# Attention over a full adjacency matrix: three bias-times-weight products on GpSimd, weight maxima by slices

## The chip, the cores and the metric

The kernel runs on one core of a Trainium2 chip. The metric is device time in microseconds (us) of one execution; lower is better.

## What is computed

```python
h = jnp.maximum(_layernorm(x, axis=-1), 0.0)
q = h @ Wq.T + bq;  k = key @ Wk.T + bk;  v = value @ Wv.T + bv
scores = jnp.einsum('nd,md->nm', q, k) / 64
adj_scores = scores * adj
adj_scores = jnp.where(jnp.abs(adj_scores) < 1e-05, -1e9, adj_scores)
prob = softmax(adj_scores, axis=-1)
out = x + jnp.einsum('nm,md->nd', prob, v) @ Wm.T + bm
```

x, key and value are 4096 x 512, adj is 4096 x 4096, the weights are 512 x 512, all fp32. The biases have 512 elements.

## The kernel before

**The algebra.** Keys and values are never projected. The start makes A = Wq^T Wk (`A_sb`) and B = Wv^T Wm^T (`B_sb`), so that a query row is h A plus a bias, multiplied directly by the keys, and an output row is (prob value) B plus a bias. Three products carry the biases: bq Wk is added to every query row (`qbias`), bk Wq is multiplied by the row (`wrow`, read by `row_dot`), bv Wm^T is added to bm (`obias`). A fourth, scalar one is bq bk (`once`, kept as `qk`). fp32 operands of the large products are split into two fp16 halves, high by ScalarE (`key_high`, `high_of`), low by VectorE (DVE; `key_low`, `low_of`), and multiplied three times (`split_product`, L559 to L561). The halves are scaled by powers of two that come from the largest element: DVE reduces each partition, TensorE flattens the column (`flat_max`), DVE reduces it again (`widest`), for keys GpSimd takes the root (`root_of`), TensorE spreads it to all partitions (`spread_max`), DVE makes the scales.

**The bias products before.** ScalarE's queue loads bq, bk, bv as columns of four per partition, and bm to all partitions (`obias`). DVE fills 12 blocks of 128 columns with repeated bias values (`bqrep`, `bkrep`, `bvrep`, L1053 to L1055), and TensorE multiplies four of them with the four 512-column slices of a weight (L695, L709, L663; L699 for the scalar). fp32 products run as two passes each, a product of four parts as eight.

**The order.** Work on every engine is written out by hand. After the start, one step t is one tile of 128 rows by 512 keys: TensorE makes the scores, DVE applies adjacency (L1225), ScalarE takes absolute values, DVE masks and keeps the maximum (L1285, L1234). Probabilities follow `LAG_P` = 9 steps later and are split, transposed by DMA (`pT`), and multiplied with the values from step `LAG_V` = 11 on. Eight steps make a block of rows, and there are 32 blocks. Steps 0 to 18 also do the rest of the preparation: the keys of groups 2 to 7 (steps 0 to 5), the transposing of Wm (`WM_STEP` 4), squares of the values on ScalarE for their maximum (up to step 7), the bv product (`BIAS_STEP` 5), B in four rounds (steps 6 to 9), the scale of values and B (`VB`, steps 7 and 8), the splitting of values (steps 8 on) and of B (`B_OUT` 10). The first product with values waits for the low half of B's first pair, since both use the bank.

**Queues.** Instructions of an engine run in the order written. SP issues nearly all loads in order, then waits for the step's events. GpSimd does `rstd_of` (three small operations for a row block), roots, the first row's units, a fourth of the values' scaling (L541) and low halves (L546), and the addition of `obias` to x (L550).

## Time and profile before

| | |
|---|---|
| runs (3) | 1592.18 us median, 1591.77 to 1592.73 |
| profiled execution | 1591.07 us |
| its span, first to last instruction | 1589.3 us |
| mean granted TensorE clock | 0.997 |
| TensorE busy | 1567.6 us, 99% |
| DVE, ScalarE, GpSimd busy | 993.6, 609.3, 101.8 us |
| DMA in the first 40 us, the next 40 us | 348, 254 GB/s |

The profile is of one execution. In the page's picture of 40 slices of 40 us, TensorE is below nine tenths in the first two slices and the last one only, and GpSimd is busy to a tenth to three tenths in slices 2 to 4 and idle elsewhere. A wait names what came last before the engine went on; "issue" is a wait that the profile can't name.

### The profile page before, as it was taken

To read this page: it belongs to the slowest core of one execution; us is meant where nothing else is said; L and a number is where in the kernel's file an instruction comes from. 1 tells how busy PE (TensorE), PEld (TensorE's weight loads), DVE (VectorE), ACT (ScalarE), POOL (GpSimd) and SP (SyncE) were. 2 spreads that over 40 slices of the span, in tenths; PEclk is the share of its full clock that TensorE was granted. 3 is DMA by queue.
4 is the path that set the end of the run, shared out by engine and by line. 5 is a ranking of instruction groups with operands and counts; after the bars stand their busy time and mean duration, and the time that the engine had idled before them with its cause. 6 is when DMAs were issued, how large, how long until landed. Compare 5 with 4: busy or idle time off the path is not lost.

```text
span 1589.3 us, 23599 instructions
## 1 busy us (share of the span) xinstructions
PE 1567.6 (99%) x7246; PEld 720.3 (45%) x7246; DVE 993.6 (63%) x2325; ACT 609.3 (38%) x964; POOL 101.8 (6%) x178
## 2 busy tenths in 40 slices
PE   8899999999999999999999999999999999999998
PEld 5543444444444444444444444444444444444443
DVE  4779766656666656656665656666566666666652
ACT  4667333333333333333333333333333333333332
POOL 0132000000000000000000000000000000000000
PEclk9999999999999999999999999999999999999999
DMA  9724555655555455555545555545555554555545
GB/s 348 254 53 107 121 130 117 130 126 125 119 125 124 116 136 119 124 125 127 117 116 137 119 123 122 130 120 119 135 123 119 121 129 119 126 129 124 116 95 106
DMA packets 430287, 205.46 MB, mean 129 GB/s; under 512 B 375088, under 2 KB 375344, under 8 KB 430128
## 3 DMA queue, kind: packets, MB, share of 16 engines
q1 hardware_dynamic: 429680, 204.80, 54.2%
q8 instruction: 16, 0.26, 0.1%
q10 hardware_dynamic: 576, 0.27, 0.1%
q14 instruction: 15, 0.12, 0.0%
HBM read 105.13 MB, written 8.39 MB: 71 GB/s over the span
## 4 chain that ended last, share of the span: by engine, by line
PE 93%; DVE 2%; DMA 2%; issue 1%; ACT 1%; SPq 1%; POOL 0%; DVEq 0%; ACTq 0%; POOLq 0%
PE R L559 13%; PE R L560 13%; PE R L561 13%; PE S L559 13%; PE S L560 13%; PE S L561 13%; PE M L559 3%; PE M L561 3%; PE M L560 3%; DMA pT<-ph 1%; PE R L638 1%; PE R L671 0%; DMA xq<-in_x_dram 0%; DVE small L1142 0%; PE W L709 0%
## 5 line engine op out<-in xcount | busy, mean ns | idle before, releaser
L941 ACT ACTIVATE drop<-Zbuf 128x512 f32<-128x512 f32 x256 | 161.2, 630 | 808.4 <-DVE cmx L1234 808.3
L1225 DVE SCALAR_TENSOR_TENSOR Zbuf<-S,rs,adjb 128x512 f32<-128x512 f32 x256 | 192.0, 750 | 346.4 <-PE S L561 342.6
L559 PE MATMUL R<-Vbuf,pT 128*128 128x512 f16 x1008 | 383.0, 380 | 6.9 <-issue 5.5
L560 PE MATMUL S<-Kbuf,qT 128*128 128x512 f16 x1024 | 388.9, 380 | 0.0
L559 PE MATMUL S<-Kbuf,qT 128*128 128x512 f16 x1024 | 388.8, 380 | 0.0
L561 PE MATMUL S<-Kbuf,qT 128*128 128x512 f16 x1024 | 388.7, 380 | 0.0
L560 PE MATMUL R<-Vbuf,pT 128*128 128x512 f16 x1008 | 382.9, 380 | 0.0
L561 PE MATMUL R<-Vbuf,pT 128*128 128x512 f16 x1008 | 382.8, 380 | 0.0
L1234 DVE CUSTOM_DVE_ANT_0 Zbuf<-drop,Zbuf 128x512 f32<-128x512 f32 x256 | 175.8, 687 | 0.0
L1285 DVE TENSOR_SCALAR drop<-drop,rs 128x512 f32<-128x512 f32 x256 | 142.1, 555 | 33.4 <-ACT drop L941 33.1
L947 ACT ACTIVATE Zbuf<-Zbuf,smx 128x1024 f32<-128x1024 f32 x128 | 157.4, 1230 | 4.5 <-DVE smx L1248 1.6
L559 PEld LDWEIGHTS R<-Vbuf,pT 128*128 128x128 f16 x1008 | 98.8, 98 | 128.0 <-issue 6.8
L559 PEld LDWEIGHTS S<-Kbuf,qT 128*128 128x128 f16 x1024 | 100.3, 98 | 121.4 <-issue 1.8
L561 PEld LDWEIGHTS S<-Kbuf,qT 128*128 128x128 f16 x1024 | 100.4, 98 | 121.3 <-issue 0.8
L560 PEld LDWEIGHTS S<-Kbuf,qT 128*128 128x128 f16 x1024 | 100.3, 98 | 121.3 <-issue 1.9
L561 PEld LDWEIGHTS R<-Vbuf,pT 128*128 128x128 f16 x1008 | 98.8, 98 | 119.6 <-issue 1.1
L560 PEld LDWEIGHTS R<-Vbuf,pT 128*128 128x128 f16 x1008 | 98.8, 98 | 118.8 <-issue 0.8
L1269 DVE SCALAR_TENSOR_TENSOR ph<-Zbuf,ph 128x512 f16<-128x512 f32 x130 | 90.0, 693 | 3.7 <-ACT ph L925 3.7
L925 ACT ACTIVATE ph<-Zbuf 128x512 f16<-128x512 f32 x130 | 81.8, 629 | 20.5 <-DMA pT<-ph 8.2
L1269 DVE SCALAR_TENSOR_TENSOR osb<-Zbuf,osb 128x512 f16<-128x512 f32 x122 | 83.4, 683 | 1.8 <-ACT osb L925 1.8
L494 POOL TENSOR_TENSOR small<-small,fixed 128x1 f32<-128x1 f32 x32 | 6.4, 201 | 1187.0 <-DVE small L989 1187.0
L925 ACT ACTIVATE osb<-Zbuf 128x512 f16<-128x512 f32 x122 | 75.0, 615 | 1.9 <-DMA pT<-osb 1.9
(189 smaller groups left out, 1194.2 us busy)
## 6 DMA issues: line engine op xcount, KB each, us to landing
adjb<-in_adj_dram SPq DMA_DIRECT2D x256, 256.0 KB, 2.8
xq<-in_x_dram SPq DMA_DIRECT2D x32, 256.0 KB, 2.8
Kbuf<-in_L_gnn_key_dram SPq DMA_DIRECT2D x8, 1024.0 KB, 14.3
xr<-in_x_dram SPq DMA_DIRECT2D x32, 256.0 KB, 2.8
out_dram<-xr SPq DMA_DIRECT2D x31, 256.0 KB, 2.3
Vbuf<-in_L_gnn_value_dram SPq DMA_DIRECT2D x7, 1024.0 KB, 8.8
pT<-ph SPq DMA_TRANSPOSE x130, 3.1
pT<-osb SPq DMA_TRANSPOSE x122, 3.1
```

Of the source, the lines that this page charges most:

```text
L494: nc.gpsimd.tensor_tensor(rstd[:, 0:1], mv[:, 1:2], eps[:, :], ALU.add).then_inc(var_ready, 1)
L559: nc.tensor.matmul(ps, lhs[0], rhs[0], start=start, stop=False)
L560: nc.tensor.matmul(ps, lhs[0], rhs[1], start=False, stop=False)
L561: return nc.tensor.matmul(ps, lhs[1], rhs[0], start=False, stop=stop)
L638: last = nc.tensor.matmul(bank_of(fill + s)[:, :], Wv_sb[:, k, s * P:(s + 1) * P], WmT[:, k, :], start=(k == 0), stop=(k == ND - 1))
L925: nc.scalar.activation(rows_p(s)[:, 0, :], probs_of(u), ACT.Copy, scale=PSCALE).then_inc(p_hi, 1)
L941: nc.scalar.activation(drop[:, :], Zbuf[:, s.p, s.c * CW:(s.c + 1) * CW], ACT.Abs).then_inc(abs_ready, 1)
L947: nc.scalar.activation(at, at, ACT.Exp, bias=smx[:, pp, 2 * NPAIR + 1:2 * NPAIR + 2], scale=smx[:, pp, NPAIR + k:NPAIR + k + 1], accum_out ...
L1225: nc.vector.scalar_tensor_tensor(out=z, in0=S[s.j % 2][:, :], scalar=rs[:, r, 3, s.c // 2:s.c // 2 + 1], in1=adjb[:, s.j % ADJ_SLOTS, :], ...
L1234: nc.vector.tensor_tensor_reduce(out=last, in0=drop[:, :], in1=last, scale=1.0, scalar=-3.4e38, op0=ALU.add, op1=ALU.max, accum_out=cmx[:, ...
L1269: nc.vector.scalar_tensor_tensor(out=rows_p(s)[:, 1, :], in0=probs_of(u), scalar=PSCALE, in1=rows_p(s)[:, 0, :], op0=ALU.mult, op1=ALU.sub ...
L1285: nc.vector.tensor_scalar(drop[:, :], drop[:, :], rs[:, r, 1, s.c // 2:s.c // 2 + 1], rs[:, r, 2, s.c // 2:s.c // 2 + 1], ALU.is_lt, ALU.m ...
```

## The change

The bias rows are loaded each as one piece of 2 KB into one partition. TensorE turns them into columns by 12 products of one column, and DVE copies these to `bqc`, `bkc`, `bvc`. For each of the three bias products GpSimd multiplies the four slices of the weight by the bias column and adds them up (`weighted_sum`: four multiplications, three additions of 128x512), and TensorE sums the result over the partitions with one product by ones (`sum_over_partitions`), which also spreads it. The scalar product is made on DVE from the columns and summed in the same way. The first sum and three slices of the second stand on GpSimd ahead of `root_of("K0")`, the last slice behind it; the third sum stands in step 5, behind DVE's reading of Wm, and writes over Wm. The bv product moves from step 5 to step 9 on TensorE, with its addition to `obias` on DVE. Warming products go from 20 to 12. DVE reads the maxima of Wq and Wk slice by slice as these land. The rest of the row preparation, and of TensorE's order in the start, is moved as the diff shows. Two adjacency loads go ahead of keys 2 to 7, and the load of bm goes from ScalarE's queue to SP's behind the first values. The diff, with declarations, renumbered fills and semaphores that follow from it left out:

```diff
-        bqrep, bkrep = [pT[:, :, :, :, :].rearrange("p a b m n -> p (a b m n)").bitcast(fp32)[:, h * ND * P:(h + 1) * ND * P]
-                        .rearrange("p (k n) -> p k n", k=ND) for h in range(2)]
-        bvrep = ph[:, :, :].rearrange("p h n -> p (h n)").bitcast(fp32).rearrange("p (k n) -> p k n", k=ND)
+
+        bias_rows = [buf[0:1, :] for buf in (drop, xr, osb)]
+        sum_q, sum_w, term = osb[:, :], xr[:, :], z1[:, 3 * 1024:3 * 1024 + D]
+        sum_o, term_o = [Wm_sb[:, k, :] for k in range(2)]
...
-        WM_STEP, BIAS_STEP, B_STEPS, B_OUT = 4, 5, {6: 0, 7: 1, 8: 2, 9: 3}, 10
+        WM_STEP, SUM_STEP, BIAS_STEP, B_STEPS, B_OUT = 4, 5, 9, {6: 0, 7: 1, 8: 2, 9: 3}, 10
...
+                if g == FIRST_KEYS:
+                    for t in range(ADJ_SLOTS):
+                        load_adj(0, t, t)
                 sp.dma_start(k_stage(g), kv[g, :, :, :]).then_inc(k_in[g], 16)
-            for t in range(ADJ_SLOTS):
-                load_adj(0, t, t)
...
             load_values([0])
+            sp.dma_start(obias[:, :], bm.partition_broadcast(P)).then_inc(bm_in, 16)
             sp.wait_ge(dot_done, 1)
...
-            rstd_of(1)
...
+            def weighted_sum(total, term, weights, k, bias, done):
+
+                nonlocal steps
+                if k == 0:
+                    nc.gpsimd.tensor_scalar(total, weights, bias[:, 0:1], None, ALU.mult).then_inc(sum_steps, 1)
+                    steps += 1
+                else:
+                    wait(pool, sum_steps, steps)
+                    nc.gpsimd.tensor_scalar(term, weights, bias[:, k:k + 1], None, ALU.mult).then_inc(sum_steps, 1)
+                    steps += 1
+                    pool.wait_ge(sum_steps, steps)
+                    last = nc.gpsimd.tensor_tensor(total, total, term, ALU.add)
+                    if k == ND - 1:
+                        last.then_inc(done, 1)
+                    else:
+                        last.then_inc(sum_steps, 1)
+                        steps += 1
+
+            pool.wait_ge(bcol, 1)
+            for k in range(ND):
+                pool.wait_ge(w_in[k], 32)
+                weighted_sum(sum_q, term, Wk_sb[:, k, :], k, bqc, q_sum)
+                if k == ND - 2:
+                    rstd_of(1)
+            pool.wait_ge(q_sum, 1)
+            for k in range(ND - 1):
+                weighted_sum(sum_w, term, Wq_sb[:, k, :], k, bkc, w_sum)
...
             root_of("K0")
+            weighted_sum(sum_w, term, Wq_sb[:, ND - 1, :], ND - 1, bkc, w_sum)
             root_of("K1")
...
+                if isinstance(s.t, int) and s.t == SUM_STEP:
+                    pool.wait_ge(wm_seen, 1)
+                    pool.wait_ge(start_act, ND)
+                    pool.wait_ge(w_sum, 1)
+                    for k in range(ND):
+                        weighted_sum(sum_o, term_o, WmT[:, k, :], k, bvc, o_sum)
...
+                    if isinstance(s.t, int) and s.b == 2:
+                        pool.wait_ge(bias_read, 1)
...
+            def sum_over_partitions(ps, part):
+
+                return nc.tensor.matmul(ps, ones.to_broadcast([P, P]), part, start=True, stop=True)
+
             def out_bias():
-                ps = bank_of(fill)
+                pe.wait_ge(o_sum, 1)
+                pe.wait_ge(v_small, 1)
                 pe.wait_ge(q_small, Q_SMALL + 1)
-                pe.wait_ge(start_act, ND)
-                for k in range(ND):
-                    last = nc.tensor.matmul(ps[:, :], bvrep[:, k, :], WmT[:, k, :], start=(k == 0), stop=(k == ND - 1))
-                filled(last)
+                sum_over_partitions(M1[:, :], sum_o).then_inc(bias_mm, 1)
...
-            for n in range(20):
+            for n in range(8):
+                nc.tensor.matmul(S[1][:, 0:P], ident[:, :], ident[:, :], start=True, stop=True)
+            pe.wait_ge(b_in, 48)
+            for n, b in enumerate(bias_rows):
+                for k in range(ND):
+                    last = nc.tensor.matmul(M0[:, n * ND + k:n * ND + k + 1], b.rearrange("a (p k) -> a k p", k=ND)[:, k, :], one,
+                                            start=True, stop=True)
+            last.then_inc(bcol_mm, 1)
+            for n in range(4):
                 nc.tensor.matmul(S[1][:, 0:P], ident[:, :], ident[:, :], start=True, stop=True)
             for k in range(ND - 1):
                 pe.wait_ge(w_in[k], 32)
                 round_a(k, range(ND))
             pe.wait_ge(w_in[ND - 1], 32)
             round_a(ND - 1, range(0, 1))
-            pe.wait_ge(ident_ready, 2)
             flat_max("A", wmax[:, 0:2], 2)
+            round_a(ND - 1, range(1, 2))
+            spread_max("A")
+            round_a(ND - 1, range(2, 3))
+            pe.wait_ge(bcol, 1)
             transpose_x(1)
-            round_a(ND - 1, range(1, 3))
-            spread_max("A")
             round_a(ND - 1, range(3, 4))
             flat_max("K0", kst[:, 6, 0:1], 1)
+            pe.wait_ge(q_sum, 1)
+            sum_over_partitions(S[1][:, :], sum_q).then_inc(aside_mm, 1)
             transpose_key(0)
             spread_max("K0")
-            pe.wait_ge(reps_ready, 1)
-            for k in range(ND):
-                last = nc.tensor.matmul(S[1][:, :], bqrep[:, k, :], Wk_sb[:, k, :], start=(k == 0), stop=(k == ND - 1))
-            last.then_inc(aside_mm, 1)
+            pe.wait_ge(bdot_ready, 2)
             pe.wait_ge(hT_ready, 1)
-            for k in range(ND):
-                last = nc.tensor.matmul(once, bqrep[:, k, :], bkc[:, k:k + 1], start=(k == 0), stop=(k == ND - 1))
-            last.then_inc(aside_mm, 1)
+            sum_over_partitions(once, bdot[:, ND:ND + 1]).then_inc(aside_mm, 1)
             pe.wait_ge(start_dve, ND)
             pe.wait_ge(k_small, 1)
             project_q(1, 0)
             transpose_key(1)
+            pe.wait_ge(w_sum, 1)
+            sum_over_partitions(wrow[:, :], sum_w).then_inc(aside_mm, 1)
             transpose_q()
             pe.wait_ge(q_small, 1)
             flat_max("K1", kst[:, 6, 1:2], 1)
-            for k in range(ND):
-                last = nc.tensor.matmul(wrow[:, :], bkrep[:, k, :], Wq_sb[:, k, :], start=(k == 0), stop=(k == ND - 1))
-            last.then_inc(aside_mm, 1)
             spread_max("K1")
...
-                        pe.wait_ge(v_small, 1)
+                        pe.wait_ge(bias_read, 1)
...
-            act.dma_start(bqc[:, :], bq.rearrange("(p k) -> p k", k=ND)).then_inc(b_in, 16)
-            act.dma_start(bkc[:, :], bk.rearrange("(p k) -> p k", k=ND)).then_inc(b_in, 16)
-            act.dma_start(bvc[:, :], bv.rearrange("(p k) -> p k", k=ND)).then_inc(b_in, 16)
-            act.dma_start(obias[:, :], bm.partition_broadcast(P)).then_inc(bm_in, 16)
+            for to, b in zip(bias_rows, (bq, bk, bv)):
+                act.dma_start(to, b.rearrange("(a d) -> a d", a=1)).then_inc(b_in, 16)
...
                 act.wait_ge(b_round, ND)
+                act.wait_ge(bias_mm, 1)
...
-            dve.wait_ge(b_in, 48)
-            dve.wait_ge(ident_ready, 2)
-            for k in range(ND):
-                nc.vector.tensor_scalar(bqrep[:, k, :], ident[:, :], 0.0, bqc[:, k:k + 1], ALU.mult, ALU.add)
-                nc.vector.tensor_scalar(bkrep[:, k, :], ident[:, :], 0.0, bkc[:, k:k + 1], ALU.mult, ALU.add)
-                last = nc.vector.tensor_scalar(bvrep[:, k, :], ident[:, :], 0.0, bvc[:, k:k + 1], ALU.mult, ALU.add)
-            last.then_inc(reps_ready, 1)
-            row_stats(1)
-            dve.wait_ge(bn_ready, 1)
-            mean_var()
-            normalise(1)
-            dve.wait_ge(rstd_ready, 1)
-            dve.wait_ge(xn_ready, 1)
-            nc.vector.tensor_scalar(xq[:, :], xq[:, :], rstd[:, 2:3], None, ALU.mult).then_inc(xs_ready, 1)
...
+            dve.wait_ge(bcol_mm, 1)
+            nc.vector.tensor_copy(small[:, 0:3 * ND], M0[:, 0:3 * ND]).then_inc(bcol, 1)
+            dve.wait_ge(bcol, 1)
+            nc.vector.tensor_tensor(bdot[:, 0:ND], bqc, bkc, ALU.mult).then_inc(bdot_ready, 1)
+            dve.wait_ge(bdot_ready, 1)
+            nc.vector.tensor_reduce(bdot[:, ND:ND + 1], bdot[:, 0:ND], X, ALU.add).then_inc(bdot_ready, 1)
             for k in range(ND):
                 dve.wait_ge(w_in[k], 32)
-            largest(0, (Wq_sb, Wk_sb)).then_inc(part_max, 1)
+                for n, w in enumerate((Wq_sb, Wk_sb)):
+                    nc.vector.tensor_reduce(wpart[:, n * ND + k:n * ND + k + 1], w[:, k, :], X, ALU.max,
+                                            apply_absolute_value=True).then_inc(w_part, 1)
+            dve.wait_ge(w_part, 2 * ND)
+            nc.vector.tensor_reduce(wmax[:, 0:2], wpart.rearrange("p (n k) -> p n k", n=2), X, ALU.max).then_inc(part_max, 1)
+            row_stats(1)
+            dve.wait_ge(bn_ready, 1)
+            mean_var()
+            normalise(1)
             widest_product("A", 2)
             scale_of(ast, a_small, "A", 400, 2.0 ** -40, 2 * TOP / D, D / (2 * TOP) / HS)
+            dve.wait_ge(rstd_ready, 1)
+            dve.wait_ge(xn_ready, 1)
+            nc.vector.tensor_scalar(xq[:, :], xq[:, :], rstd[:, 2:3], None, ALU.mult).then_inc(xs_ready, 1)
             dve.wait_ge(k_sum, 2)
...
                 dve.wait_ge(bm_in, 16)
-                dve.wait_ge(start_mm, fill + 1)
-                nc.vector.tensor_tensor(obias[:, :], bank_of(fill)[:, :], obias[:, :], ALU.add).then_inc(start_dve, 1)
-                fill += 1
+                dve.wait_ge(bias_mm, 1)
+                nc.vector.tensor_tensor(obias[:, :], M1[:, :], obias[:, :], ALU.add).then_inc(bias_read, 1)
...
-                        dve.wait_ge(start_mm, FILLS.index("bias") + 1)
+                        dve.wait_ge(o_sum, 1)
...
-                        largest(2, (Wm_sb,))
+                        largest(2, (Wm_sb,)).then_inc(wm_seen, 1)
```

## Rows read from the trace of the kernel before

**Rows 1.** The page: busy us, share of span, instructions of each engine.

```profile
PE 1567.6 (99%) x7246; PEld 720.3 (45%) x7246; DVE 993.6 (63%) x2325; ACT 609.3 (38%) x964; POOL 101.8 (6%) x178
```

**Rows 2.** What TensorE waited for, 0 to 200 us: total, times, longest.

```profile
PE R L559 <- issue: 5.5, 1, 5.5
...
PE M L603 <- POOL gmax L504: 3.5, 2, 2.8
...
PE M L559 <- DMA ho<-row: 0.9, 1, 0.9
```

**Rows 3.** Timeline (start, us, engine, line): TensorE's four products, one A product.

```profile
10.29 1.02 PE L627 MATMUL S<-Zbuf 128*128 128x512 f32 x2
...
29.43 3.70 PE L695 MATMUL S<-Zbuf,pT 128*128 128x512 f32 x8
...
32.96 0.95 PE L699 MATMUL R<-small,pT 128*128 128x1 f32 x8
...
40.08 3.70 PE L709 MATMUL W<-Zbuf,pT 128*128 128x512 f32 x8
...
83.30 3.60 PE L663 MATMUL M<-Zbuf,ph 128*128 128x512 f32 x8
```

**Rows 4.** Warming products (timeline), then two bias loads (issues: us to landing).

```profile
1.71 6.17 PE L678 MATMUL S<-ident 128*128 128x128 f32 x40 [1.71 <-POOL ident L488]
...
small<-in_L_gnn_bq_dram ACTq DMA_DIRECT2D x1, 2.0 KB, 3.4
...
small<-in_L_gnn_bv_dram ACTq DMA_DIRECT2D x1, 2.0 KB, 6.1
```

**Rows 5.** Timeline of DVE: a maximum over 512 columns.

```profile
37.35 0.69 DVE L1011 TENSOR_REDUCE small<-row 128x1 f32<-128x512 f32 x1
```

**Rows 6.** Timeline, 20 to 29 us: weights' maximum, its spread, K0's root.

```profile
20.14 0.60 PE L595 MATMUL M<-ident,small 128*1 128x128 f32 x4 [1.10 <-DVE small L1142]
...
22.97 0.38 PE L603 MATMUL M<-gmax,fixed 1*128 1x1 f32 x2
...
28.52 0.55 POOL L504 TENSOR_TENSOR gmax<-gmax,fixed 1x1 f32<-1x1 f32 x1 [13.44 <-DVE gmax L1070]
```

**Rows 7.** Lines of GpSimd: ns min/median/max of 128x512 multiplication and addition.

```profile
L541 POOL TENSOR_SCALAR Vbuf<-Vbuf,small x6: 1560/1650/2092, 107.9 to 116.6; 128x512 f32<-128x512 f32 x6
...
L550 POOL TENSOR_TENSOR xr<-xr,obias x32: 1264/1294/1567, 168.3 to 1579.6; 128x512 f32<-128x512 f32 x32
```

**Rows 8.** Timeline, 36 to 47 us: key square, `q_high`, K2's maximum.

```profile
36.11 1.91 ACT L848 ACTIVATE Zbuf<-Kbuf 128x2048 bf16<-128x2048 f32 x1
...
39.87 0.60 ACT L815 ACTIVATE qT<-R 128x512 f16<-128x512 f32 x1 [1.76 <-PE R L587]
...
45.60 0.15 DVE L1103 TENSOR_REDUCE kst<-small 128x1 f32<-128x2 f32 x1
...
46.71 0.38 PE L595 MATMUL M<-ident,kst 128*1 128x128 f32 x2
```

**Rows 9.** Timeline, 88 to 103 us: DVE, GpSimd and TensorE, steps 5 to 8.

```profile
88.16 0.68 DVE L1198 TENSOR_TENSOR obias<-M,obias 128x512 f32<-128x512 f32 x1
...
88.76 2.27 DVE L1142 TENSOR_REDUCE small<-B_sb 128x1 f32<-128x2048 f32 x1
...
98.34 0.16 DVE L1263 TENSOR_REDUCE small<-small 128x1 f32<-128x10 f32 x1 [0.68 <-ACT pT L897]
...
100.36 0.56 POOL L504 TENSOR_TENSOR gmax<-gmax,fixed 1x1 f32<-1x1 f32 x1 [29.59 <-DVE gmax L1070]
...
102.34 0.38 PE L603 MATMUL M<-gmax,fixed 1*128 1x2 f32 x2
```

**Rows 10.** Timeline of DVE: low halves of B.

```profile
121.72 2.47 DVE L1136 SCALAR_TENSOR_TENSOR B_sb<-R,small,B_sb 128x1024 f16<-128x1024 f32 x2
```

**Rows 11.** Stretch 25 to 30 us: busy by engine, clock, DMA share, GB/s.

```profile
25.00:30.00 5.00, 3.42 (x20) 2.30 (x21) 3.84 (x10) 4.01 (x6) 0.55 (x1) 1.00 1.06 388
```

**Rows 12.** Stretch 63 to 64 us: TensorE's busy time and granted clock.

```profile
63.00:64.00 1.00, 1.00 (x4) 0.50 1.03 358
```

More of the change, by code:

```diff
@@ L100, in adjacency_attention @@
         mhalf, half, hscale, eps, ounit, qk = [fixed[:, k:k + 1] for k in (0, 1, 3, 4, 5, 6)]
-        halves, one = fixed[:, 1:3], fixed[0:1, 7:8]
+        halves, ones, one = fixed[:, 1:3], fixed[:, 7:8], fixed[0:1, 7:8]
         rs = sb("rs", [P, 2, 4, NPAIR])
@@ L484, in _ @@
             pool.memset(eps[:, :], EPS)
-            pool.memset(one, 1.0)
+            pool.memset(ones, 1.0)
             pool.memset(ident[:, :], 0.0).then_inc(ident_ready, 1)
@@ L933, in step @@
                     if s.t == B_OUT:
-                        skip_bias()
                         high_b()
@@ L1126, in low_of @@
                 nonlocal fill
-                dve.wait_ge(start_hi, sum(f not in ("Wm^T", "bias") for f in FILLS[:fill + 1]))
+                dve.wait_ge(start_hi, sum(f != "Wm^T" for f in FILLS[:fill + 1]))
                 nc.vector.scalar_tensor_tensor(out=low, in0=bank_of(fill)[:, :], scalar=scale, in1=high,
@@ L1134, in low_of_pair @@
                 nonlocal fill
-                dve.wait_ge(start_hi, sum(f not in ("Wm^T", "bias") for f in FILLS[:fill + 2]))
+                dve.wait_ge(start_hi, sum(f != "Wm^T" for f in FILLS[:fill + 2]))
                 nc.vector.scalar_tensor_tensor(out=low, in0=pair_of_banks(fill), scalar=scale, in1=high,
```

25 lines of the change are left out of this document (10 added, 15 removed).

## Prediction

> **What bounds the kernel now.** I read the page first: TensorE is busy 99% of the span [rows 1]. Then TensorE's waits, which say where the remaining per cent is: 5.5 us once ahead of the first probabilities-times-values product, 2.8 us once ahead of the spread of a key maximum, 0.9 us ahead of a product from `ho`, and nothing else of weight [rows 2]. All of it lies before 175 us. After that TensorE never waits, and the change touches nothing there. So the question is only by how much the last of these waits, at 173 us, ends earlier; everything behind it moves with it. TensorE time removed before 175 us counts only where TensorE, and not another engine's chain, decides what comes next. So I followed the chain of work in order of time through the start and priced the change at each place where the chain meets it.
>
> **TensorE time removed.** A product of four 128x512 fp32 parts is eight passes and takes 3.60 to 3.70 us; the change takes out three of them, and the scalar one of 0.95 us [rows 3]. Each comes back as one product by ones of two passes (1.02 us on its own, 0.43 us a pass in a row, so 0.86), the scalar one as two small passes of 0.12. That is 3 x 2.75 + 0.7 = 9.0 us less for TensorE in the first 90 us. How much of it reaches 173 us?
>
> **Start, up to the first key maximum.** TensorE's warming products go from 20 to 8, then come 12 products of one column that turn the three bias rows into columns (24 small passes), then 4 more warming products. Twenty warming products took 6.17 us from 1.71 on, so eight end at about 4.3 [rows 4]. The bias rows are then awaited. Before, the last bias landed 6.1 us after its issue at 1.66, at 7.8, in 128 pieces of 16 bytes [rows 4]; the new rows are one piece of 2 KB each. The lower bound is the 3.4 us of the first such load, the upper one 7.8. I take 4.6, near the lower, because the pieces are few. The 24 small passes cost 0.12 each by the scalar product's row (2.9 us; 0.2 each at a slower clock, 5.1), and the copy on DVE with its semaphores about 0.4 (an estimate, under the 0.69 of a 512-column DVE reduction [rows 5]). So the bias columns are there at 8.0 (7.0 to 11.5), and the first product of weights starts at 8.3 instead of 7.7. The maxima of the weights by slices are eight reductions of 0.69 [rows 5] from 8.2 on, as the slices land, done by about 14, where the two long ones ended at 20.1 and made TensorE wait 1.1 us [rows 6]. Now the thirteenth product of round A is last, about 19.5. The spread of A's maxima moves ahead of the transposes of x and of one product, so it comes at about 21.5 instead of 22.97 [rows 6]: the chain of DVE and ScalarE that splits A, and with it the widest key maximum, could come 1.4 us earlier, at about 27.1 instead of 28.52 [rows 6].
>
> **GpSimd's sums decide there.** `root_of("K0")` now stands behind the whole sum for bq and three quarters of the one for bk. Prices: the nearest row for the multiplication is 1.56 us at least, 1.65 median, 2.09 at most; for the addition 1.26 to 1.57 [rows 7]. I take the lower ends, since what DVE does beside it at that time mostly reads one SBUF tile or PSUM. With 0.08 us from one to the next, a slice costs 1.56 + 0.08 + 1.26 + 0.08 = 2.98. Sum for bq: 1.6 + 3 x 2.98 = 10.6, and `rstd_of(1)` inside it, three ops of at most 0.55 like the root's, 1.5: done at 8.0 + 12.1 = 20.1, before TensorE asks for it at about 25. Three slices of the other: 1.6 + 2 x 2.98 = 7.6, so the root starts at 27.7. That is 0.8 us earlier than before, not 1.4. At GpSimd's upper prices (seven multiplications 0.53 dearer, five additions 0.31) it starts at 33.0, which is 4.5 later than before.
>
> The Trainium skill speaks against putting such work on GpSimd (GPSIMD Engine Reference, section 4.1, Engine selection): elementwise work on a tile belongs on VectorE, an operation with two inputs being about twice as slow, while one with a single input runs roughly at line rate. The rows disagree with the second half: here the one-input multiplication is the slower one, 1.56 against 1.26. By the page the multiplications would halve and the sums would drop off the chain; the sum below would gain 0.6 us at most.
>
> **From there to the first scores: 2.4 us more.** Before, TensorE did the bq product (3.70) and the scalar one (0.95) between the spread of K0 and `project_q(1)`, and ScalarE had to wait for both. Now `project_q(1)` is over before DVE has split the first keys. What is late next is DVE's split, then ScalarE: after K0's scale it does four `key_high`, two small copies, and two squares of keys, 1.91 us each plus their accumulator reads [rows 8], and only then `q_high`. Following these durations from 27.7, ScalarE is free at 36.7; `q_high` stood at 39.87 [rows 8]. So that is 3.2 earlier: 0.8 from before and 2.4 here.
>
> **The bk product, 0.9 us.** Its 3.70 us on TensorE lay between the maximum of K1 and its spread [rows 3]. DVE was busy with `key_low(1)` just as long anyway, and its `row_dot` gains nothing of its own. Scores of step 0 could end 1.7 earlier, but the maximum of K2 that TensorE needs next is made on DVE after K1's scales, at 45.60 plus 0.15, where TensorE asked at 46.71 [rows 8]: 0.9 is gained. Then key splits on ScalarE and DVE lead, and all are earlier by 3.2 + 0.9 = 4.1 up to step 5.
>
> **Steps 5 to 9: nothing, -0.1.** The bv product's 3.60 us falls out of TensorE's order at 83.30 [rows 3]. But ScalarE squares the values one after the other without a break until 98.3; only then does DVE make their maximum, at 98.34 [rows 9], and TensorE waits for it. So TensorE only idles. GpSimd's third sum starts when DVE has read Wm, 91.0 less the 0.6 of the bias addition that has left its front [rows 9]. It lasts 1.7 + 3 x 3.1 = 11.0 (prices in the middle of their rows, DVE being busy), ends at 101.4 in the old clock of events, and `root_of("VB")`, at 100.36 before, goes at 101.4 to 102.0; TensorE's spread moves from 102.34 [rows 9] to about 102.4. Bounds: 0.4 gained, 2.5 lost.
>
> **Step 9: -0.7.** From 109 to 123 DVE works without a wait worth naming (values, row preparation, then the low half of B) and TensorE waits 5.5 us for the first pair of B's low halves, which DVE starts at 121.72 [rows 10]. The change moves the addition to `obias`, 0.68 us [rows 9], from step 5 into this stretch. The product by ones in step 9 (0.86) hides in that wait.
>
> Nothing else is on a path: the two adjacency tiles ahead of six key loads, 0.5 MB at 388 GB/s [rows 11], delay keys by 1.3 us, and ScalarE reaches each key some us after it lands; `obias` now comes by SP behind the first values and is read in step 9. GpSimd's additions to `xr` wait for `bias_read` long after it is set.
>
> **Sum.** 0.8 + 2.4 + 0.9 - 0.1 - 0.7 = 3.3 us. The profiled span is 1589.3 and that execution took 1591.07, so 1.8 lie around it; the sum gives a span of 1586.0 and an execution of 1587.8. The median of the runs shown is 1592.18, 1.1 above that execution; 3.3 off it is 1588.9, which I predict.
>
> **The rivals.**
> The clock. With the bk product gone, TensorE sits idle before the first scores for between 2 and 3.7 us. After the idle 2.8 us ahead of the K3 spread, the granted clock fell to 0.50, which is 1.2 GHz, for over three microseconds [rows 12]. Scores of step 0 would then take up to 1.8 us more, of which 0.8 is absorbed by the wait for K2's maximum: 1.0 lost, so 1589.9. Shorter idles (1.1 us at 20.1) were followed by no fall. The one-column products at the start may have the same effect.
>
> GpSimd too slow, the rival on the other side. From a start of the K0 root later than 27.7 + 3.3 = 31.0 on, the kernel is slower than before. At the upper prices the root is 5.3 later than I take it (gain 3.3 down to -2.0), and the third sum holds the VB root, losing up to 2.5 more: 1596.7. Against it: DVE seldom uses two SBUF tiles then. The skill's rule is harsher (SBUF — State Buffer, section "SBUF: two separate sides"): the port pair shared by the two is locked for a whole instruction, and the loser fully blocks. The spread of 1.56 to 2.09 in this trace agrees in kind.
>
> Bias rows late. If they land near 7.8, the columns and GpSimd's sums start 3 us later: gain 0.3, 1591.9.
>
> All of it counts. If the values' squares and the split chain weren't binding, the whole 9.0 less 2.9 for the columns and 0.7: 5.4, 1586.8.
>
> **How the numbers follow.** Forecast as summed (gain 2.9 to 3.9): 0.43. Clock: 0.25. Late or otherwise half lost (0.3 to 2): 0.15. More than 3.9, up to 5.4: 0.10. Slower: 0.07. The range that leaves out no more than two in ten is 1586.5 to 1592.3. A measurement of this kernel can tell about 0.2%, 3.2 us, from no change. The forecast lies on that bound: of its 0.43 I give 0.30 to above it. Faster by over 0.2%: 0.30 + 0.10 = 0.40; within: 0.13 + 0.25 + 0.15 = 0.53; slower: 0.07.
>
> **What would show it.** In the changed trace: bias columns read by DVE near 8; GpSimd's first sum done near 20 and the K0 root near 27.7 right behind an addition, multiplications of 1.56; `q_high` at 36.7; TensorE idle before scores 0 with granted clock 1.00 or 0.50; the spread of VB 4 us earlier than 102.34, released by GpSimd; the first pair of B's low halves 3.3 us earlier than 121.72, and the `ho` wait near 173 too. I am wrong if GpSimd's ops there exceed 1.8, if the clock stays low beyond one stretch, or if the values' squares, tied to loads, don't move with the rest.

## The result and the profile after

The changed kernel takes 1595.75 us (median of 17 runs, 1594.24 to 1597.62), the kernel before 1592.23 (17 runs, 1590.59 to 1594.47). The ratio is 1.0024, with a 95% interval of 1.0018 to 1.0031: 3.5 us slower, where 3.3 us faster was forecast. The time lies outside the range of 1586.5 to 1592.3.

| | before | after |
|---|---|---|
| median | 1592.23 | 1595.75 |
| profiled execution | 1591.07 | 1595.81 |
| its span | 1589.3 | 1593.8 |
| its mean granted clock | 0.997 | 0.995 |

The page after, first the busy times (answering to [rows 1]), then the line of TensorE's clock in 40 slices:

```profile
PE 1568.3 (98%) x7230; PEld 722.3 (45%) x7230; DVE 993.9 (62%) x2323; ACT 609.1 (38%) x964; POOL 132.9 (8%) x199
...
PEclk9899999999999999999999999999999999999999
```

TensorE is busy as long as before, although 9 us of products were to go. GpSimd has 31 us more, as meant. What TensorE waited for in the first 200 us, beside [rows 2]:

```profile
PE R L600 <- issue: 4.8, 1, 4.8
PE M L644 <- POOL gmax L536: 2.7, 1, 2.7
PE M L644 <- DVE Kbuf L1153: 2.1, 1, 2.1
...
PE M L600 <- DMA ho<-row: 1.5, 1, 1.5
PE M L636 <- DVE small L1303: 1.3, 1, 1.3
PE R L628 <- DVE row L1060: 1.2, 1, 1.2
```

No new wait is long enough to explain it. The timeline of TensorE in the first 16 us of the changed kernel (start, us, engine, line, operation) shows the first loss:

```profile
1.69 3.78 PE L721 MATMUL S<-ident 128*128 128x128 f32 x16 [1.69 <-POOL ident L491]
5.40 2.02 PE L725 MATMUL R<-fixed,drop 1*128 1x1 f32 x8
7.29 2.00 PE L725 MATMUL R<-fixed,xr 1*128 1x1 f32 x8
9.15 2.00 PE L725 MATMUL R<-fixed,osb 1*128 1x1 f32 x8
11.08 2.07 PE L729 MATMUL S<-ident 128*128 128x128 f32 x8
12.95 3.52 PE L668 MATMUL R<-Zbuf 128*128 128x512 f32 x6
```

The 24 small passes (two for each one-column product) last 5.7 us (5.40 to 11.08), 0.24 each and not 0.12. The four warming products behind them take 0.23 a pass. Round A, the products of the first weights, starts at 12.95 instead of 7.71, its first two passes slow as well (0.85 and 0.79 us apart, then 0.43). The second loss stands at the first scores, in the changed kernel:

```profile
43.12 0.58 PE L644 MATMUL M<-gmax,fixed 1*128 1x1 f32 x2 [2.09 <-DVE Kbuf L1153]
...
43.63 0.61 PE L600 MATMUL S<-Kbuf,qT 128*128 128x512 f16 x1
...
48.30 0.55 PE L602 MATMUL S<-Kbuf,qT 128*128 128x512 f16 x1
48.78 0.38 PE L636 MATMUL M<-ident,kst 128*1 128x128 f32 x2
```

A product of the scores starts every 0.43 us where it was 0.22 before, and K2's maximum is at 48.78 (46.71 in [rows 8]). The stretches of the same trace (the length, the busy time of TensorE, of its weight loads, of DVE, ScalarE and GpSimd, then the granted clock, the DMA share and GB/s):

```profile
40.00:42.00 2.00, 0.96 (x6) 0.51 (x6) 0.52 (x3) 2.00 (x5) 0.00 (x0) 0.95 0.99 366
42.00:44.00 2.00, 0.88 (x3) 0.63 (x4) 2.00 (x5) 2.00 (x5) 0.55 (x1) 0.50 0.16 60
44.00:46.00 2.00, 2.00 (x6) 0.76 (x5) 1.89 (x6) 1.91 (x3) 0.00 (x0) 0.50 0.03 11
```

This table gives the start of the same event in each trace, in us (e1, f5 and the others are the experiments below):

| | before | after | e1 | f5 | e3 | f1 | f3 | g1 |
|---|---|---|---|---|---|---|---|---|
| round A, first product | 7.71 | 12.95 | 8.91 | 8.91 | 12.95 | 8.17 | 7.84 | 6.75 |
| A's maximum on TensorE | 20.14 | 24.98 | 20.17 | 20.17 | 24.73 | 19.43 | 20.79 | 18.01 |
| K0's root on GpSimd | 28.52 | 32.17 | 27.83 | 27.30 | 32.15 | 26.95 | 28.00 | 25.98 |
| `q_high` | 39.87 | 40.95 | 36.61 | 38.66 | 40.93 | 35.67 | 36.77 | 34.70 |
| scores 0 | 44.02 | 43.63 | 39.28 | 42.80 | 43.41 | 38.15 | 39.46 | 37.18 |
| scores 0 read by DVE | 46.88 | 48.95 | 44.68 | 45.66 | 47.58 | 42.74 | 44.85 | 41.35 |
| K3's root | 61.78 | 63.84 | 59.72 | 60.56 | 61.85 | 57.01 | 60.01 | 55.62 |
| VB's largest on DVE | 98.34 | 100.78 | 96.79 | 97.12 | 100.06 | 95.21 | 95.26 | 92.37 |
| VB's root | 100.36 | 103.64 | 99.65 | 99.14 | 102.92 | 98.07 | 98.12 | 95.23 |
| low halves of B | 121.72 | 124.12 | 120.18 | 120.51 | 123.41 | 118.59 | 118.91 | 116.03 |

The changed kernel has won back the 5.2 us by the scores, which start 0.4 us earlier than before. Then they run at half the clock, and from their start to K3's root it takes 20.2 us instead of 17.8.

### The profile page after: what moved, and what is told of

Its sections match the earlier page's. It is cut to its first block, busy times and chain, and to the rows that moved or that the text cites. A ratio compares the mean times of both kernels' runs of the same rounds, so it can differ in the third digit from the quotient of the medians.

```text
span 1593.8 us, 23590 instructions
## 1 busy us (share of the span) xinstructions
PE 1568.3 (98%) x7230; PEld 722.3 (45%) x7230; DVE 993.9 (62%) x2323; ACT 609.1 (38%) x964; POOL 132.9 (8%) x199
## 4 chain that ended last, share of the span: by engine, by line
PE 93%; DVE 2%; DMA 2%; issue 1%; ACT 1%; SPq 0%; POOL 0%; DVEq 0%; ACTq 0%; POOLq 0%
PE R L600 13%; PE R L602 13%; PE R L601 13%; PE S L600 13%; PE S L601 13%; PE S L602 13%; PE M L600 3%; PE M L602 3%; PE M L601 3%; DMA pT<-ph 1%; PE R L679 1%; PE R L668 1%; DMA ho<-row 0%; PE R L725 0%; DVE Kbuf L1161 0%
```

## The experiments

Times of the kernel before in the three groups of runs: 1592.14 us (27 runs) beside the e kernels, 1592.31 (34) beside f1 to f4, 1592.69 (24) beside g1 to g3 and f5. The diffs are against the changed kernel unless another is named.

**e1: the bias columns by DMA again.** The sums on GpSimd and the slices stay.

```
-            for n in range(8):
...
-            pe.wait_ge(b_in, 48)
-            for n, b in enumerate(bias_rows):
...
-            for n in range(4):
+            for n in range(20):
...
-                act.dma_start(to, b.rearrange("(a d) -> a d", a=1)).then_inc(b_in, 16)
+                act.dma_start(to[:, :], b.rearrange("(p k) -> p k", k=ND)).then_inc(b_in, 16)
```

> The changed kernel with one part undone: the biases come as columns by DMA as before, the 12 products of one column are gone, and TensorE makes 20 warming products again. Theory (the column products delay everything): the first product of weights starts at 7.7 us instead of 12.95, the K0 root on GpSimd at about 27.5 instead of 32.2, and the time falls by 3 to 5 us below the changed kernel, to about 1592 or under. Rival (GpSimd's sums stand in the way): the K0 root follows an addition without a gap and the time falls by no more than 1 us. A second rival (the clock falls in the new idle stretch before the first scores): at most 2 us are gained, and the granted clock is 0.50 around those scores.

Measured: 1590.4 us (1588.67 to 1591.45, 11 runs), ratio to before 0.9987 (0.9978 to 0.9996). The column products cost 5.3 us of the median, more than the whole deficit.

**e2: the column products behind the first products of weights,** so that TensorE runs fast when it comes to them.

```
+                if k == 0:
+                    pe.wait_ge(b_in, 48)
+                    for n, b in enumerate(bias_rows):
...
```

> The changed kernel with the 12 column products moved behind the first four products of weights; 20 warming products as before the change. Tells what the column products cost when TensorE runs at full clock: if their 0.24 us a pass comes from the slow clock at the start, the 24 passes take 2.6 to 2.9 us there and round A ends 2.5 us later than before the change instead of 5; if it is their own price, they take 5.7 us again. Time: 2 us below the changed kernel in the first case, 0 to 1 in the second.

Measured: 1599.72 us (1599.23 to 1600.7, 5 runs), ratio 1.0048 (1.0034 to 1.0061). That is 4.0 above the changed kernel, where I had expected it 0 to 2 below. TensorE's timeline in this run, then two stretches with the clock:

```profile
8.24 2.74 PE L668 MATMUL R<-Zbuf 128*128 128x512 f32 x6
...
11.78 2.02 PE L729 MATMUL R<-fixed,drop 1*128 1x1 f32 x8
...
17.46 5.49 PE L668 MATMUL R<-Zbuf 128*128 128x512 f32 x6
```

```profile
14.00:16.00 2.00, 2.00 (x11) 2.00 (x10) 0.00 (x0) 0.62 (x1) 0.00 (x0) 1.00 1.05 387
18.00:20.00 2.00, 2.00 (x3) 0.66 (x2) 2.00 (x5) 1.91 (x2) 1.83 (x2) 0.50 1.06 388
```

The small passes cost 0.24 (11.78 to 17.46) also right behind products at the fast rate (0.43 a pass), and at a granted clock of 1.00. The price is their own. The clock falls to 0.50 at 16.1, while the last of them run, and the six passes of weights behind them take twice as long (5.49 us for 2.74), although the profile shows TensorE busy throughout. K0's root is at 37.25, 5.1 later than in the changed kernel.

**f4: contiguous blocks of the bias rows as weights.** The biases' elements stand in another order, the one part of the computation that differs.

```
-   b.rearrange("a (p k) -> a k p", k=ND)[:, k, :]
+   b[:, k * P:(k + 1) * P]
```

> The changed kernel with blocks of 128 contiguous elements of each bias row as the weights of the twelve one-column products, in place of every fourth element; the elements of the biases so stand in another order, which is the one part of the computation that differs. If the stride is what makes a pass 0.24 us, the 24 passes take 0.12 each as the prediction had it: 2.9 us instead of 5.7, round A 2.8 us earlier and the time near 1593. If 0.24 is the price of loading 128 columns of weights for one product, the stage and the time stay: 12.95 us for round A, 1595.7.

Measured: 1592.84 us (1590.42 to 1595.95, 11 runs), 2.9 under the changed kernel; ratio to before 1.0004 (0.9995 to 1.0012). Its TensorE:

```profile
5.40 1.20 PE L725 MATMUL R<-fixed,drop 1*128 1x1 f32 x8
6.47 1.03 PE L725 MATMUL R<-fixed,xr 1*128 1x1 f32 x8
7.36 1.03 PE L725 MATMUL R<-fixed,osb 1*128 1x1 f32 x8
8.32 1.34 PE L729 MATMUL S<-ident 128*128 128x128 f32 x8
9.45 4.30 PE L668 MATMUL R<-Zbuf 128*128 128x512 f32 x6
```

With the stride of four elements gone a pass takes 0.12 (5.40 to 8.32), the price that the prediction had. The clean comparison is with e2, where TensorE ran at the fast rate too: 0.24. What contiguous weights cost at the slow rate, at which the changed kernel's columns ran, is not shown, since f4 leaves that rate at about 5.8 us. The scalar product of [rows 3] has contiguous weights; that is why it did not show this. Even here round A starts at half the clock (4.30 for six passes in place of 2.74; the granted clock is 0.50 from 10 to 12 us).

The Trainium skill has the rule that I passed over (SBUF — State Buffer, section "Door 1: The DMA port swizzle"): an access that crosses into another 16-byte line pays, and four fp32 elements fill a line, so a stride of four takes a new line for every element. The trace agrees in kind: 0.24 a pass against 0.12. f3 limits that agreement.

**f3: the three bias rows as one tile of three partitions, and four transposes** of 3x128 in place of the twelve products.

```
-            for n, b in enumerate(bias_rows):
-                for k in range(ND):
-                    last = nc.tensor.matmul(M0[:, n * ND + k:n * ND + k + 1], b.rearrange(...)[:, k, :], one, ...)
+            for k in range(ND):
+                last = nc.tensor.transpose(M0[:, 3 * k:3 * k + 3],
+                                           drop[0:3, :].rearrange("a (p k) -> a k p", k=ND)[:, k, :], ident[0:3, 0:3])
```

> The changed kernel with the three bias rows in partitions 0 to 2 of one tile, and four transposes of 3x128 elements in place of the twelve one-column products: 8 passes instead of 24 if a transpose of float32 takes two, 4 if it takes one. If every small pass costs the 0.24 us that the 24 took, whatever its shape, the stage falls from 5.7 us to 1.0 to 1.9, round A begins 3.8 to 4.7 us earlier (12.95 to between 8.3 and 9.2) and the time is 1591 to 1592. If the price lies in the strided read of each row (every fourth element) and grows with the rows read, the stage stays at 1.9 to 3 us and the time at 1592 to 1593. If the lateness of round A came from the landing of the rows and not from the passes, nothing changes: 1595.7.

Measured: 1587.96 us (1585.8 to 1590.14, 10 runs), ratio to before 0.9975 (0.9965 to 0.9984), 7.8 us under the changed kernel.

```profile
5.40 0.64 PE L724 MATMUL R<-ident,drop 3*128 3x3 f32 x4
5.97 2.08 PE L728 MATMUL S<-ident 128*128 128x128 f32 x8
7.84 4.44 PE L668 MATMUL R<-Zbuf 128*128 128x512 f32 x6
```

0.6 us (5.40 to 5.97) do what took 5.7: four passes instead of 24, and 0.14 each although the stride is the same. So the stride alone is not dear; the stride in a two-pass fp32 product is. What makes the difference between the two forms is open. The gain is larger than the 3.8 to 4.7 that was expected. K3's root comes 3.8 us earlier than in the changed kernel, VB's largest 5.5: between them the clock stays at 1.00, where it falls in the kernels before and after. 1.8 us more are gained between the low halves of B and `project_q(4)` (at 176.8 in the changed kernel, 169.8 here). 0.8 of them lie in a fall of the clock that every trace here has, at the wait for the first product with values. The fall lasts 6.8 us in before, after, e1, e2, e3, f1, f2 and f5, and 3.4 in e4, f3, f4 and g1 to g3; from the low halves of B to `project_q(3)` it takes 6.2 to 6.5 us in the first and 5.4 to 5.7 in the others. TensorE from 5.0 to 6.4 us behind the start of the low halves, in the changed kernel, then in f3:

```profile
129.10:130.50 1.40, 1.40 (x4) 0.50 0.56 164
```

```profile
123.90:125.30 1.40, 1.40 (x8) 1.00 0.51 162
```

The rest is shorter waits of TensorE up to `project_q(4)`, 1.1 us in f3 and 1.9 in the changed kernel, most of them for `ho`. Why the fall is short in some kernels is open.

**e3: seven idle products of 128x128 ahead of the spread of K1's maxima,** where TensorE sits idle in the changed kernel.

```
             flat_max("K1", kst[:, 6, 1:2], 1)
+            pe.wait_ge(start_dve, reads(last_fill(0), False))
+            for n in range(7):
+                nc.tensor.matmul(S[0][:, 0:P], ident[:, :], ident[:, :], start=True, stop=True)
             spread_max("K1")
```

> The changed kernel with seven 128x128 products that nobody reads between the flattening and the spread of K1's maximum, where TensorE idles 2.1 us. Theory of the clock: the granted clock stays at 1.00, the first scores take 2.6 us instead of 5.1, and the time falls by 1.8 to 2.1 us. Rival (scores 0 have slack, since GpSimd's units of the first row are late anyway): no more than 0.5 us.

Measured: 1592.83 us (1590.69 to 1595.54, 11 runs), ratio 1.0001 (0.9992 to 1.001). The granted clock stays at 1.00 from 34 to 60 us, from scores 0 to K3's root it takes 18.4 us (after: 20.2), and the kernel is 2.9 us faster than the changed one for doing more work. The clock is a cause of its own. Its size is less sure than its sign: of the 2.0 us at K3's root the trace keeps 0.7 at the low halves of B (123.41 against 124.12). The fall at K3 lasts 6.8 us here and 3.4 in the changed kernel, and from K3's root to VB's largest it takes 38.2 us in the three traces with the long fall (e3, f1, f2), 36.6 to 37.1 in the six with the short one.

**f5: only the slices, on the kernel before:** maxima of the weights slice by slice, row preparation behind them, transposes of x behind round A. No sums on GpSimd.

```
-            largest(0, (Wq_sb, Wk_sb)).then_inc(part_max, 1)
+                for n, w in enumerate((Wq_sb, Wk_sb)):
+                    nc.vector.tensor_reduce(wpart[:, n * ND + k:n * ND + k + 1], w[:, k, :], X, ALU.max, ...)
+            nc.vector.tensor_reduce(wmax[:, 0:2], wpart.rearrange("p (n k) -> p n k", n=2), X, ALU.max).then_inc(part_max, 1)
```

> The kernel before with the maxima of the first weights read slice by slice and the order of the first stage that goes with it (row preparation behind the maxima, transposes of x behind round A), and without any of the sums on GpSimd: biases by DMA, products of the biases by weights as before. The prediction had 0.8 us from the earlier start of K0's root, and 2.4 from the bias products leaving TensorE's queue ahead of q_high. By that the run has K0's root at 27.7 to 28.0 us, q_high 0 to 0.8 us earlier than 39.87, and 1591.4 to 1592.2. If most of what the run with DMA columns gained by q_high (3.3 us) belongs to the slices, it comes at 36.6 here and the time is near 1590.

Measured: 1590.65 us (1589.53 to 1591.7, 11 runs), ratio 0.9986 (0.9977 to 0.9995). K0's root comes 1.2 us earlier than before. Between K0's root and `q_high` lie 11.4 us as before; in e1 they are 8.8. So the sums on GpSimd do give the 2.4 us that were forecast (2.6), and 3.5 at the scores (39.28 against 42.80). At K3's root 0.8 of them are left, and e1 with the sums (1590.4) is no faster than f5 without (1590.65). The stretches 42 to 44 us of e1 and of the kernel before say why:

```profile
42.00:44.00 2.00, 2.00 (x7) 0.60 (x4) 0.77 (x8) 1.48 (x2) 1.56 (x7) 0.50 0.44 168
```

```profile
42.00:44.00 2.00, 2.00 (x7) 0.76 (x5) 2.00 (x5) 2.00 (x3) 0.00 (x0) 1.00 0.14 53
```

In the second TensorE is in the bk product, which stands between K1's maximum and its spread and keeps it at work. Without that product it waits and the clock falls to 0.50. From scores 0 to K3's root it takes 20.4 us in e1, 17.8 in f5 and before. With the clock held, in e3 and f1, it takes 18.4 and 18.9: the clock has 1.6 to 1.8 of it. The rest, 0.7 to 1.1, I put down to the chain of DVE and ScalarE, which TensorE now reaches earlier; no run shows that by itself.

**f1: e1 with the idle products of e3.**

```
+            for n in range(7):
+                nc.tensor.matmul(S[0][:, 0:P], ident[:, :], ident[:, :], start=True, stop=True)
```

> The bias columns are brought by the DMAs of the kernel before, as in the run that did only this (1590.4 us), and seven idle products of 128x128 stand ahead of the spread of K1's maxima, as in the run with only these (1592.8). If the two causes are independent, the gain of the idle products (1595.75 - 1592.8 = 2.9) comes off 1590.4: 1587.5 us, with a granted clock of 1.00 from round A to scores 0, scores 0 at 0.32 us a product and z0 about 2 us earlier than the 44.7 us of the run with the DMAs alone. If the clock fell only because TensorE had been slow and late at the start, the idle products change nothing any more: 1590.4.

Measured: 1588.98 us (1587.84 to 1590.78, 11 runs), ratio 0.9984 (0.9975 to 0.9993): 1.4 under e1 by the medians, half of what e3 gained; the intervals overlap, so that this gain is likely and not shown. The clock held at scores 0 falls one wait later, behind the 2.74 us for K3's root:

```profile
54.00:58.00 4.00, 1.26 (x10) 1.02 (x8) 3.61 (x8) 2.63 (x3) 2.90 (x9) 0.87 1.05 398
58.00:62.00 4.00, 4.00 (x11) 1.50 (x12) 2.29 (x4) 0.72 (x1) 0.00 (x0) 0.50 1.04 373
```

From K3's root to the transposes behind scores 3 it takes 6.2 us (57.01 to 63.23), in f3 3.5 (60.01 to 63.53).

**g1 and g2: f3 with the idle products at K1, g1 also with nine at K3.** The part that is in g1 alone:

```
                     if s.t == 2:
+                        wait(pe, z1_ready, 2)
+                        for n in range(9):
+                            nc.tensor.matmul(S[1][:, 0:P], ident[:, :], ident[:, :], start=True, stop=True)
                         spread_max("K3")
```

> The changed kernel with the four 3x128 transposes in place of the column products (1587.96 us), with seven idle products ahead of the spread of K1's maxima and nine ahead of the spread of K3's. In the run with the transposes alone the granted clock is 0.50 from 39 to 45 us (scores 0 to z0 5.4 us instead of 2.9 in the kernel before) and 1.00 at K3 (60.6 to 66). If each fall of the clock has its cause in the idle stretch before it, both stretches stay at 1.00 and the time falls by 2.1 to 2.5 us: 1585.7. If a fall that is held off comes at the next idle stretch whatever stands in it, the clock is 0.50 from 58 to 64 and the time 1587.5 to 1588.5.

> The same without the nine idle products at K3. In the run with DMA columns and seven idle products the clock fell at K3's spread instead (0.50 from 57.7 to 63.3; from K3's root to the transposes behind scores 3 it took 6.2 us instead of 3.5). If that repeats, the gain of 2.1 us at scores 0 is lost again at K3: 1588.0 to 1588.6, and the run above is 2 to 3 us faster than this one. If not, 1585.7 as the run above.

Measured: g1 1586.31 us (1585.09 to 1587.31, 5 runs), ratio 0.9957 (0.9943 to 0.9971); g2 1588.26 (1585.53 to 1590.15, 8 runs), ratio 0.9966 (0.9956 to 0.9977). g1's clock in its profiled execution, at the two places:

```profile
36.00:40.00 4.00, 3.61 (x19) 1.73 (x18) 3.86 (x11) 3.91 (x6) 0.61 (x2) 1.00 1.02 404
...
58.00:62.00 4.00, 4.00 (x29) 2.79 (x27) 2.80 (x11) 1.56 (x2) 0.23 (x1) 1.00 1.04 384
```

The theory of the idle stretches gave 1585.7 for g1. g2 did not lose the clock at K3, as I had expected, but at 28 to 32 us, where no other trace has a fall. So where an idle stretch costs the clock differs from one execution to the next, and the two intervals overlap: that the nine products at K3 add anything to f3 with seven is not shown. Nor is a gain of the seven by themselves: g2 is f3 with them, and its median is no lower (1588.26 and 1587.96), although scores 0 are read 2.4 us earlier. g1 is the fastest kernel here, 6.4 us under the one before.

**g3: the kernel before with nine idle products at K3.** The same lines as in g1, ahead of K3's spread.

> The kernel before with nine idle products ahead of the spread of K3's maxima alone. Its clock is 0.50 from 62.6 to 66.2 us: from K3's root (61.78) to the transposes behind scores 3 (66.98) it took 5.2 us, where the run with the transposes, at 1.00, took 3.5. If the idle stretch is the cause, this kernel gains 1.7 us and is at 1590.5; then the kernel before also paid for the clock, and the two changes must be compared without it. If it changes nothing, 1592.2.

Measured: 1591.76 us (1590.13 to 1592.62, 11 runs), ratio 0.9994 (0.9985 to 1.0003). The clock is 1.00 where it was 0.50 in [rows 12], and the low halves of B come 1.3 us earlier (120.43). The medians differ by 0.9, which the interval doesn't part from nothing. All eleven executions have a mean clock of at least 0.998. Of the kernel before's 24, those at 0.998 or more take 1589.8 to 1592.1 us, those at 0.995 or 0.996 1593.4 to 1594.8. Its profiled execution (1591.07, 0.997) lies between them by its clock.

**e4: the addition to `obias` one step later,** away from the stretch ahead of the low halves of B.

```
-                    if s.t == BIAS_STEP:
+                    if s.t == BIAS_STEP + 1:
                         add_bias()
```

> The changed kernel with DVE's addition to obias one step later, behind the low halves of B. If that addition lies on DVE's chain up to the first product with values, as I summed it, that product starts 0.6 us earlier against the values' maximum, and the time falls by 0.7 us, which five rounds hardly tell from nothing; if the chain has slack, nothing moves.

Measured: 1595.7 us (1592.27 to 1597.31, 11 runs), ratio 1.002 (1.0011 to 1.0029): no difference to the changed kernel. The addition did stand there (`117.09 0.68 DVE L1239` in the trace of after). But from VB's spread to the low halves it takes 19.53 us in after, 19.43 in e4 and 19.38 before: its cost was 0.10 to 0.15, not 0.68.

**f2: f1 with e4's edit, and the last slice of the third sum behind VB's root.**

```
-                    for k in range(ND):
+                    for k in range(ND - 1):
                         weighted_sum(sum_o, term_o, WmT[:, k, :], k, bvc, o_sum)
...
                         root_of("VB")
+                        weighted_sum(sum_o, term_o, WmT[:, ND - 1, :], ND - 1, bvc, o_sum)
```

> The kernel with the DMA columns and the idle products, with two more edits in the steps 5 to 9: the last slice of GpSimd's third sum (a product of 1.56 us and an addition of 1.26) follows the root of VB instead of standing ahead of it, and the addition of obias stands one step later. If GpSimd's last addition (102.4 to 103.6 us in the changed kernel) is what the root of VB waits for, the root comes 0.9 to 2 us earlier and the time falls by 0.5 to 1.5 us against the run without the two edits: about 1586.5. If VectorE's part of VB is the wait and GpSimd's sum beside it only stretches it, the place of the sum changes nothing on the path: no difference beyond 0.3 us.

Measured: median 1588.82 us (1587.38 to 1591.52, 11 runs; a twelfth took 3358.95 and is left out), ratio 0.998 (0.9971 to 0.9989): no difference to f1. VB's root comes 1.0 us earlier (97.07 against 98.07), its spread 0.06 (98.95 against 99.01). The spread stands behind the twelve products of a step's scores in TensorE's queue, and the last of these starts at 98.64. The root is not what comes last there.

## Why the prediction was wrong

**The step that failed: the price of the bias columns.** "The 24 small passes cost 0.12 each by the scalar product's row (2.9 us; 0.2 each at a slower clock, 5.1)". They cost 0.24 each at either clock, 5.7 us. The row that I took is a one-column product too, over 128 partitions instead of one, but its weights are contiguous and it ran at the fast rate. The stride in the diff's `rearrange` makes the price twice as high at that rate (0.24 in e2, 0.12 in f4), and neither of my bounds covered it, though the upper one, 5.1 for a slower clock, missed by only 0.6. Of the 4.65 us by which round A is later than the forecast 8.3, 2.8 are in these passes, 0.8 ahead of them (5.40 for 4.6), and 1.1 in the four warming products behind them, which still ran at the slow rate.

**An average used for its first part.** I let eight warming products end at 4.3 by dividing the 6.17 us of [rows 4] by twenty. They ended at 5.4, in the kernel after and in f3. The group has two rates, by the starts of its passes one every 0.21 us at first and one every 0.11 later. The two stretches touch 6 and 11 passes, those across their ends counted:

```profile
3.00:4.00 1.00, 1.00 (x6) 1.00 (x6) 1.00 0.84 248
...
6.00:7.00 1.00, 1.00 (x11) 1.00 (x11) 1.00 1.01 289
```

These are stretches of 1 us of the kernel before, for its warming products alone. I should have split the group. The bias rows were hardly awaited, if at all (the first column product at 5.40 has no wait on its line), so the rival of late rows falls.

**GpSimd's sums: the prices right, their place on the path in part.** In the changed kernel (GpSimd's timeline):

```profile
23.30 1.56 POOL L509 TENSOR_SCALAR xr<-Zbuf,small 128x512 f32<-128x512 f32 x1
24.95 1.56 POOL L513 TENSOR_SCALAR Zbuf<-Zbuf,small 128x512 f32<-128x512 f32 x1
26.60 1.26 POOL L516 TENSOR_TENSOR xr<-xr,Zbuf 128x512 f32<-128x512 f32 x1
...
32.17 0.56 POOL L536 TENSOR_TENSOR gmax<-gmax,fixed 1x1 f32<-1x1 f32 x1 [1.23 <-DVE gmax L1095]
```

Priced at 12.1 and 7.6 us, the sum for bq and the three slices of the other took 11.8 (11.46 to 23.30) and 7.6 (23.30 to 30.94). They end 1.2 us before K0's root is ready, so the rival of a slow GpSimd falls too. In e1, with the columns in time, the root goes at 27.83 (forecast 27.7), but there too it has waited 1.2 us for DVE's maximum: I had the sums come last, so that this agreement is partly luck. In f1 and g1 the root goes right behind an addition (26.95 and 25.98), and there the sums decide. The one-input multiplication stays dearer than the addition (1.56 against 1.26), against what the Trainium skill states (GPSIMD Engine Reference, section 4.1, as in the prediction).

**The gain in the start: right.** From K0's root to `q_high` I had 9.0 us; after and e1 both show 8.8, before and f5 11.4. With the start repaired and the clock held (f1), K3's root comes 4.8 earlier than before, where the sum had 4.1.

**The clock: a rival at 0.25 with a loss of 1.0, and it is the second cause.** The idle is at the low end of what I named (2.09 us), yet the clock fell: the scores take 5.2 us instead of 2.6, 2.0 are lost at K3's root (63.84 after, 61.85 in e3), 2.9 in the median. I had named 1.8 for the slower scores, from too few products, and 0.8 of it as absorbed. What I had no term for is the fall at K3 [rows 12]. It was in the kernel before as a given, but it comes and goes: it is in the profiled executions of before, after, e1 to e4, f1, f2 and f5, and not in those of f3, f4 and g2, although f3 waits there as long (2.75 us). I also passed over the longest fall of the kernel before, 0.50 from 120.8 to 127.6 us behind the idle of 5.5, which the changed kernel has as well (123.7 to 130.6).

**Steps 5 to 9: the size right, the reason not.** I forecast -0.1. From DVE's largest for VB to the spread it takes 4.00 us before and 3.81 after. GpSimd's last addition does hold the root (103.64, 2.9 behind the largest, where it was 2.0), but f2 shows that the spread waits for the scores in TensorE's queue anyway. Nor are the squares of the values tied to loads: in g1, VB's largest comes 6.0 us earlier.

**Step 9: -0.7 forecast, 0.15 measured** (e4). DVE had slack ahead of the low halves that its busy line hides.

**Together:** the gains of e1 (5.3 us, the columns) and e3 (2.9, the clock at K1) don't add up: f1, which has both, is 6.8 under the changed kernel. Less its deficit of 3.5, that leaves 3.3 for everything else, where 3.3 was forecast, and f1 is at 1588.98 where I had 1588.9. Part of that is luck: K0's root comes 1.6 earlier than before (forecast 0.8) and step 9 costs 0.15 (forecast 0.7), while f1's fall at K3 lasts 6.8 us and that of the kernel before 3.4. g1, with cheaper columns and no fall at K1 or K3, is at 1586.31.

Not settled: from `project_q(3)` to `project_q(4)` the traces take between 45.1 us (before) and 46.9 (e4), after 46.2. Without TensorE's waits all take 44.2 to 44.4. The waits are 0.9 us before and 1.9 after: 1.5 for `ho`, where it was 0.9, and 0.3 for a low half of the values by GpSimd. About 1 us of after's deficit in its profiled execution lies there. g3, whose code is the same there as in the kernel before, waits 1.4, so no run tells how much of it belongs to the change. Nor does a run take back the moved adjacency loads or the later load of bm by themselves: they are among the 3.3 us of everything else.

## What to carry over

Price a small operation by a row with the same access pattern, not only the same shape, and look whether a group in the profile mixes two rates before dividing it. Work that is taken from TensorE ahead of a wait makes the wait longer, and what follows may then run at half the clock: before counting such a gain, look at what the granted clock did behind each idle stretch (here it fell at waits of 2.1 and 2.7 us, and in f3 it held at one of 2.75). Where it falls, try a few idle products in the gap: they took 2.9 us off the changed kernel (e3), while in f1 and g2 no gain is clear of noise. One trace shows one execution: the same fall lasted 3.4 us in some and 6.8 in others.

## What the runs showed of the hardware

- A pass of a one-column fp32 product whose 128 weights stand four elements apart takes 0.24 us, at the fast rate (e2) and at the slow one (after); with contiguous weights 0.12 at the fast rate (f4). A transpose of 3x128 with the same stride takes 0.14 (f3).
- In e2 the granted clock fell to 0.50, which is 1.2 GHz, at 16.1 us, 4.3 us into a row of such products, and in f4 at 9.2 us, behind 2.9 us of one-column products with contiguous weights and the warming products that follow, though TensorE was busy without a break in both.
- At the start TensorE begins a pass of the warming products every 0.21 us and later every 0.11, while the column of the granted clock reads 1.00 for both. The fast rate comes at 4.8 to 7.3 us in the seven kernels that have only warming products there (before, e1, e2, f1, f2, f5, g3), and at 14.0 to 17.2 in the three with the strided column products among them (after, e3, e4). It differs between executions: round A begins at 8.91 in e1 and at 8.17 in f1, whose first instructions are the same. The Trainium skill says both (TensorE: Matmul & The Clock Gate, section "Part 1: The HAM clock gate"): throttled is the default state, and the moment of the change varies from run to run.
- A DVE operation on SBUF tiles beside a GpSimd sum was stretched to more than twice its 0.68 us, and the multiplication behind it from 1.56 to 1.88, in the changed kernel:

```profile
99.21 1.64 DVE L1274 CUSTOM_DVE_ANT_0 Zbuf<-drop,Zbuf 128x512 f32<-128x512 f32 x1
100.40 1.88 POOL L513 TENSOR_SCALAR B_sb<-Zbuf,small 128x512 f32<-128x512 f32 x1
```
